# First attention: one bank pair for scores, two for transposed scores, values once per pair of heads

## The reference, cut to what matters

```python
h = concatenate([tokens(x), txt], axis=1)
h = h + attention16(layernorm(h))        # the stage that is changed most
h = h + recurrence(layernorm(h))         # gated recurrence over the batches, in order
h = h + gated_scan(layernorm(h));  h = h + quantised_mlp(layernorm(h))
h = h + masked_attention(layernorm(h));  h = h + top1_experts(layernorm(h))
h = h + alibi_attention(layernorm(h));   h = h + capacity_experts(layernorm(h))

# the first attention: 16 heads of width 16
xn = layernorm(x) * g + b
q, k, v = xn @ Wq + bq, xn @ Wk + bk, xn @ Wv + bv
attn = einsum('bnhd,bmhd->bnmh', q, k) / sqrt(16)
y = einsum('bnmh,bmhd->bnhd', softmax(attn, axis=2), v)
```

## Time and profile before

| | us |
|---|---|
| median of 3 runs | 2595.54 |
| lowest, highest run | 2593.53, 2599.7 |
| profiled execution, its time | 2592.93 |
| profiled execution, its span | 2591.0 |
| first attention, main loop | 207.6 to 638.2 |
| TensorE busy, share of the span | 1877.0 (72%) |
| DVE busy, share of the span | 1153.2 (45%) |
| TensorE clock granted, mean over the span | 0.886 |

### The profile page before, as it was taken

How to read it: one execution, slowest core, us unless ns; L and a number is a source line. 1 busy time by engine, 2 the same in 40 slices (tenths; PEclk the granted TensorE clock), 3 DMA queues, 4 the chain that set the end, 5 groups by cost and what they waited for, 6 DMA issues and landing times. The chain is left out here.

```text
span 2591.0 us, 33680 instructions
## 1 busy us (share of the span) xinstructions
PE 1877.0 (72%) x9606; PEld 1224.2 (47%) x9607; DVE 1153.2 (45%) x3544; ACT 750.1 (29%) x1842; POOL 487.2 (19%) x631
## 2 busy tenths in 40 slices
PE   0026399998995857876885299970899998984798
PEld 0013144443664546654554166650466665663576
DVE  2434276676225556654443011115566565661111
ACT  0002144444321102211221022210666555660221
POOL 0020010010001022210002500005344343452012
PEclk9999699999998979877995599995799888996899
DMA  9224455351002000003000400004000000001342
GB/s 199 76 47 143 99 102 91 64 106 22 0 0 55 0 0 1 0 1 162 0 0 0 150 29 28 28 21 134 1 7 18 14 15 15 17 18 35 108 141 78
DMA packets 75136, 131.23 MB, mean 51 GB/s; under 512 B 25670, under 2 KB 63202, under 8 KB 70686
## 3 DMA queue, kind: packets, MB, share of 16 engines
q1 hardware_dynamic: 49786, 106.58, 16.2%
q0 software_dynamic: 20512, 14.29, 2.4%
q10 hardware_dynamic: 4722, 9.09, 1.2%
HBM read 90.74 MB, written 40.13 MB: 51 GB/s over the span
## 5 line engine op out<-in xcount | busy, mean ns | idle before, releaser
L2117 POOL TENSOR_SCALAR l_P<-l_P,l_ri 111x111 f32<-111x111 f32 (+1 forms) x256 | 179.9, 721 | 232.9 <-DVE l_ri L2294 232.6
L622 ACT ACTIVATE PT<-psT 111x666 f32<-111x666 f32 x192 | 139.4, 726 | 220.3 <-PE psT L703 219.9
L523 DVE TENSOR_REDUCE mx<-psS 111x2 f32<-111x666 f32 x192 | 159.8, 848 | 88.2 <-PE psS L688 88.1
L2384 ACT ACTIVATE l_P<-l_S,l_nm 111x111 f32<-111x111 f32 (+2 forms) x384 | 179.2, 472 | 30.3 <-DVE l_nm L2287 30.0
L1231 PE MATMUL q_psY<-q_wq,q_xT 128*111 128x256 f32 x576 | 153.8, 426 | 2.1 <-ACT q_xT L1190 1.6
L714 PE MATMUL psO<-PT,vS 111*32 111x333 f32 x768 | 149.0, 467 | 0.1
L2504 PE MATMUL l_psP<-ident,l_P 111*111 111x111 f32 x768 | 108.1, 280 | 40.9 <-DVE l_PT L2303 39.8
L1827 DVE COPY t_hT<-t_psG 128x512 f32<-128x512 f32 x56 | 36.1, 686 | 214.3 <-PE t_psG L1869 214.3
L2504 PEld LDWEIGHTS l_psP<-ident,l_P 111*111 111x111 f32 x768 | 93.9, 187 | 71.9 <-DVE l_PT L2303 42.1
L1231 PEld LDWEIGHTS q_psY<-q_wq,q_xT 128*111 128x111 f32 x576 | 112.7, 202 | 31.0 <-issue 2.5
L1880 PE MATMUL t_psY<-expert_w,t_hT 128*128 x448 | 105.5, 389 | 18.6 <-DVE t_hT L1827 18.6
(11 more groups left out here) (378 smaller groups left out, 3697.8 us busy)
## 6 DMA issues: line engine op xcount, KB each, us to landing
expert_w<-in_moe_dram SPq DMA_DIRECT2D x8, 2048.0 KB, 15.1
c_w<-in_moe_dram SPq DMA_DIRECT2D x16, 1024.0 KB, 7.2
qs<-halves_scratch SPq DMA_DIRECT2D x128, 83.5 KB, 3.3
ks<-halves_scratch SPq DMA_DIRECT2D x128, 83.5 KB, 4.2
halves_scratch<-high SPq DMA_DIRECT2D x32, 167.0 KB, 4.1
halves_scratch<-low SPq DMA_DIRECT2D x32, 167.0 KB, 4.7
c_xb<-xs_scratch SPq DMA_DIRECT2D x8, 667.3 KB
xs_scratch<-zeros SPq DMA_DIRECT2D x6, 777.0 KB
```

The lines of the kernel that those rows point to most:

```text
L523: v.tensor_reduce(mx[J % 2][:, t, c:c + 65:64], psS[s % 2][0:TT, :, 0:T], AX.X, ALU.max, negate=True).then_inc(max_done, 1)
L622: s_.activation(PT[jp % 2][:, :, a, :], psT[0:TT, :, 0:T], ACT.Exp).then_inc(exp_done, 1)
L2117: r = g.tensor_scalar(Pt, Pt, ri[:, c % 2, 2 * t + half:2 * t + half + 1], None, ALU.mult)
L2384: s_.activation(P[c % 4][:, half, at(t):at(t + 1)], Sm[:, half, at(t):at(t + 1)], ACT.Exp, bias=nm[:, c % 2, i:i + 1], scale=-1.0, accum_o ...
```

## The change

The edit has five parts.
1. In the first attention the six banks of scores are shared out anew: one pair for scores, two for transposed scores. Scores of step s now wait for the maximum of step s - 1, and transposed scores of step s for the exponential of step s - 2.
2. `values` is called once for each pair, at steps with s % 3 = 1, for all three tiles of the pair before.
3. `AT` is written anew so that pieces stand at s % 3 = 1 (ahead of the transposed scores) and s % 3 = 2 (behind them), on TensorE and on ScalarE. `oS` has two buffers, and its copy comes a step later.
4. The zeros, their memset and their DMAs move to `recurrence`.
5. In the ALiBi attention the list of pieces is reordered, `route_rows` moves behind the pieces of chunk 4, and a drain is added ahead of `batch_stats`.

```diff
@@ attention16
-        oS = sb("oS", [128, T])
+        oS = [sb(f"oS{i}", [128, T]) for i in range(2)]
-        zeros = sb("zeros", [128, 1792])
-        psS = [pb2(f"psS{i}") for i in range(2)]
-        psT = pb2("psT")
+        ps = [pb2(f"ps{i}") for i in range(3)]
...
-        AT = [(1, "x", 0), (2, "x", 1), (3, "qk", 0), (4, "qk", 1), (5, "most", 1), (6, "ot", 3), (7, "qk", 2),
-              (8, "qk", 3), (9, "ot", 0), (11, "most", 2), (12, "v", 0), (13, "v", 1), (15, "ot", 1), (17, "most", 3),
-              (21, "ot", 2), (23, "most", 0)]
+        AT = [(1, "x", 0), (2, "x", 1), (4, "most", 1), (5, "qk", 0), (7, "qk", 1), (8, "ot", 3), (10, "most", 2),
+              (11, "ot", 0), (13, "qk", 2), (14, "qk", 3), (16, "most", 3), (17, "ot", 1), (19, "v", 0), (20, "v", 1),
+              (22, "most", 0), (23, "ot", 2)]
...
+        def score_bank(s):
+            return ps[0]
+        def less_bank(s):
+            return ps[1 + s % 2]
@@ SP
             batch(0, 0)
-            sync.wait_ge(zeros_ready, 1)
-            n = 0
-            for f in fills:
...
-            sync.wait_ge(filled, n)
@@ ScalarE
-                    if s == 1 and not first:
+                    if s == 2 and not first:
                         out(b - 1, 3)
-                    if s % 6 == 1 and s > 1:
+                    if s % 6 == 2 and s > 2:
                         out(b, s // 6 - 1)
-                    for args in pieces(b, p, s, first, last):
-                        piece(*args)
+                    if s % NT == 1:
+                        for args in pieces(b, p, s, first, last):
+                            piece(*args)
                     exp(b, s)
+                    if s % NT != 1:
+                        for args in pieces(b, p, s, first, last):
+                            piece(*args)
@@ TensorE
-                if some(NS * b + s - 1):
-                    pe.wait_ge(max_done, NS * b + s - 1)
+                if some(NS * b + s):
+                    pe.wait_ge(max_done, NS * b + s)
...
-                if some(NS * b + s):
-                    pe.wait_ge(exp_done, NS * b + s)
+                if some(NS * b + s - 1):
+                    pe.wait_ge(exp_done, NS * b + s - 1)
...
-            def values(b, p, s):
-                jp, a = s // NT, s % NT
-                pe.wait_ge(exp_done, NS * b + s + 1)
-                if s % 6 == 0 and some(4 * b + jp // 2):
+            def values(b, p, jp):
+                pe.wait_ge(exp_done, NS * b + NT * jp + NT)
+                if jp % 2 == 0 and some(4 * b + jp // 2):
                     pe.wait_ge(o_out, 4 * b + jp // 2)
-                for half in range(2):
...
-                if a == NT - 1:
-                    r.then_inc(pv_done, 1)
+                for a in range(NT):
+                    for half in range(2):
...
+                r.then_inc(pv_done, 1)
...
                     if s + AHEAD < NS or not last:
                         scores(*of(b, p, s + AHEAD))
-                    if s >= 2:
-                        values(b, p, s - 2)
-                    elif not first:
-                        values(b - 1, 1 - p, NS + s - 2)
-                    for args in pieces(b, p, s, first, last):
-                        piece(*args)
+                    if s % NT == 1:
+                        if s > NT:
+                            values(b, p, s // NT - 1)
+                        elif not first:
+                            values(b - 1, 1 - p, NPAIR - 1)
+                        for args in pieces(b, p, s, first, last):
+                            piece(*args)
                     scores_less_most(b, p, s, first, last)
+                    if s % NT != 1:
+                        for args in pieces(b, p, s, first, last):
+                            piece(*args)
@@ recurrence
+            nc.gpsimd.memset(zeros[:, :], 0.0).then_inc(zeros_ready, 1)
+        @block.sync
+        def _(sync):
+            sync.wait_ge(zeros_ready, 1)
+            n = 0
+            for f in fills:
...
+            sync.wait_ge(filled, n)
@@ alibi_attention
-        AT = [(0, "x", 0), (1, "x", 1), (2, "k", 0), (3, "k", 1), (4, "q", 0), (5, "out", 0), (6, "q", 1),
-              (7, "out", 1), (8, "q", 2), (9, "out", 2), (10, "q", 3), (12, "q", 4), (13, "v", 0), (14, "rx", 0),
-              (15, "rx", 1), (16, "rl", 0), (17, "v", 1), (18, "rk", 0), (19, "q", 5), (20, "v", 2), (21, "q", 6),
-              (22, "q", 7)]
+        AT = [(0, "x", 0), (1, "x", 1), (2, "k", 0), (3, "k", 1), (4, "out", 0), (5, "q", 0), (7, "out", 1),
+              (8, "q", 1), (10, "out", 2), (11, "q", 2), (12, "q", 3), (13, "v", 0), (14, "q", 4), (15, "rx", 0),
+              (16, "rx", 1), (17, "rl", 0), (18, "q", 5), (19, "v", 1), (20, "rk", 0), (21, "q", 6), (22, "v", 2),
+              (23, "q", 7)]
...
-                    if c == 4 and not first:
-                        route_rows(b - 1)
...
                     if c == 3 and not first:
+                        dve.drain()
                         batch_stats(nc, dve, sh, b - 1).then_inc(h_done, 1)
+                    if c == 4 and not first:
+                        route_rows(b - 1)
```

More of the change, by code:

```diff
@@ L323, in token_scale, with attention16 @@
     g.tensor_tensor(r, r, b, ALU.mult).then_inc(done, 1)
-def attention16(nc, sh, fills):
+def attention16(nc, sh):
     H, DH = 16, 16
@@ L490, in _ @@
             c.then_inc(consts, 1)
-            g.memset(zeros[:, :], 0.0).then_inc(zeros_ready, 1)
             def lower(b, n):
@@ L522, in largest @@
                 dve.wait_ge(s_done, NS * b + s + 1)
-                v.tensor_reduce(mx[J % 2][:, t, c:c + 65:64], psS[s % 2][0:TT, :, 0:T], AX.X, ALU.max,
+                v.tensor_reduce(mx[J % 2][:, t, c:c + 65:64], score_bank(s)[0:TT, :, 0:T], AX.X, ALU.max,
                                 negate=True).then_inc(max_done, 1)
@@ L674, in piece @@
                     for t in range(NT):
-                        r = nc.tensor.transpose(psM[0:TT, 128 * t:128 * t + 128], oS[:, qt(t)], sh.ident[:, :])
+                        r = nc.tensor.transpose(psM[0:TT, 128 * t:128 * t + 128], oS[j % 2][:, qt(t)], sh.ident[:, :])
                 r.then_inc(piece_done, 1)
@@ L683, in scores @@
                         pe.wait_ge(stack_in[n], 128 * (b + 1))
-                if some(NS * b + s - 1):
-                    pe.wait_ge(max_done, NS * b + s - 1)
+                if some(NS * b + s):
+                    pe.wait_ge(max_done, NS * b + s)
                 for half in range(2):
                     ph = slice(64 * half, 64 * half + 64)
-                    r = mm(psS[s % 2][0:TT, half, 0:TE], qs[p][ph, jp, qt(t)], ks[p][ph, jp, :], start=True, stop=True)
+                    r = mm(score_bank(s)[0:TT, half, 0:TE], qs[p][ph, jp, qt(t)], ks[p][ph, jp, :], start=True, stop=True)
                 r.then_inc(s_done, 1)
@@ L730, in body, with recurrence @@
                         scores(*of(b, p, s + AHEAD))
-                    if s >= 2:
-                        values(b, p, s - 2)
-                    elif not first:
-                        values(b - 1, 1 - p, NS + s - 2)
-                    for args in pieces(b, p, s, first, last):
-                        piece(*args)
+                    if s % NT == 1:
[5 more added lines that the diff above has]
+                            piece(*args)
                     scores_less_most(b, p, s, first, last)
+                    if s % NT != 1:
+                        for args in pieces(b, p, s, first, last):
+                            piece(*args)
                 if last:
-                    values(b, p, NS - 2)
-                    values(b, p, NS - 1)
+                    values(b, p, NPAIR - 1)
                     piece(*tail())
             batches(pe, body)
-def recurrence(nc, sh):
+def recurrence(nc, sh, fills):
     with ExitStack() as ctx:
@@ L759, in recurrence @@
         ps_tmp = sb("r_tmp", [TT, 2, NTILES])
+        zeros = sb("r_zeros", [128, 1792])
+        zeros_ready, filled = sem("r_zeros_ready"), sem("r_filled")
         ps = [pb(f"r_ps{i}") for i in range(8)]
@@ L771, in _ @@
             token_scale(nc, pool, sh, ps_tmp, "plain", scaled)
+            nc.gpsimd.memset(zeros[:, :], 0.0).then_inc(zeros_ready, 1)
[4 more added lines that the diff above has]
+            for f in fills:
+                parts = 128 if f.shape[0] % 128 == 0 else TT
+                flat = f.rearrange("(p r) c -> p (r c)", p=parts)
+                for a in range(0, flat.shape[1], 1792):
+                    m = min(1792, flat.shape[1] - a)
+                    sync.dma_start(flat[:, a:a + m], zeros[0:parts, 0:m]).then_inc(filled, 16)
+                    n += 16
+            sync.wait_ge(filled, n)
         @block.vector
@@ L2760, in program @@
             tokenise(nc, sh, ins, h0)
-            attention16(nc, sh, [xs, xs2[0:E * CAP, :]])
-            recurrence(nc, sh)
+            attention16(nc, sh)
+            recurrence(nc, sh, [xs, xs2[0:E * CAP, :]])
```

20 lines of the change are left out of this document (10 added, 10 removed).

## The result

The changed kernel takes 2642.09 us (median of 4 runs, 2640.1 to 2647.5) against 2594.53 for the kernel before beside it (4 runs, 2587.2 to 2599.7). The ratio is 1.0189, with a 95% interval of 1.0159 to 1.0218: 48 us slower, where 2656 was forecast. The profiled execution took 2647.5 us with a span of 2645.5, so against that of before it is 54.5 longer.

A forecast was written before the change was run, and what follows sets the result against it. TensorE was taken to bound the first attention before, the scores-maximum chain after. First attention +43, clock +27 and ALiBi -10 gave +60: 2653 us for the profiled execution, 2656 for the median, range 2600 to 2705.

The forecast's parts named there:

- The bound and the hole: First attention: TensorE bounds a middle batch of 45.5 us; the 59.9 us hole from SP's zero writes goes, at cost 0.
- One bank pair, the walk of the groups: First attention: scores wait for the preceding step's maximum; groups of three steps sum to 59.4 us a batch against 45.5.
- The loop ends: First attention: at three loop ends DVE stands 2.83 us before the norm, now on the path: +8.4 us.
- The clock: First attention: TensorE's idle gaps lower its clock, 3.4 us of low level twice a batch, 1.7 lost each: +27 us.
- The whole of the first attention: The stage takes 473.4 us against 430.6, +43, and the clock's fall adds +27.
- The ALiBi attention: Later router rows and reordered pieces gain 0.6 us a batch, 2.3 with a clock fall: -10, bounds +5 and -33.
- The sum: Whole kernel: +43 + 27 - 10 = +60 us, 2653 for the profiled execution and 2656 for the median.
- Rival 1: First attention: the scores chain binds but the clock stays up: +33, 2629 us; chance 0.18.
- Rival 2: First attention: clock as in the quantised stage (+46) and stacks late by 4 us a batch (+28): 2703 us; chance 0.16.
- Rival 3: First attention: DVE's work fits under the values block, TensorE's 42 us sets the batch: 2508 us; chance 0.13 including half-way.
- Its other leg: First attention: one values block in place of three is a gain, since changing the tiling mode drains TensorE; 1.9 against 2.22 us.
- Rival 4: Recurrence: nothing of the zeros is won, since their writes block that stage; they would have to last over 175 us there.

The follow-up runs named there:

- run 1: The kernel before with only the zeros, their memset and their DMAs moved to the recurrence: 2528.44 us, ratio 0.9762.
- Runs 6: version 3 with one bank pair for scores and its wait as the only further edit: 2550.32 us, ratio 0.9839.
- run 7: The changed kernel with the old list of places (`AT`) in the first attention; banks, waits and values block as changed: 2576.86 us, ratio 0.9931.
- run 9: The changed kernel with one more VectorE memset behind the maximum at each step with s % 3 = 2: 2656.21 us, ratio 1.0261.
- run 8: The kernel before with only `route_rows` moved behind the pieces of chunk 4 in the ALiBi attention: 2600.75 us, ratio 1.0024.
- run 12: version 3 with values once for each pair of heads and the copy of the result one step later: 2530.93 us, ratio 0.9778.
- version 3: The kernel before with the zeros moved and the ALiBi edit, the first attention's order as before: 2503.67 us, ratio 0.9647.
- run 4: The changed kernel with two bank pairs for scores and one for transposed scores again; values once per pair and places as changed: 2557.37 us, ratio 0.9863.

## Why the prediction was right, point by point

**The bound and the hole: right.** The 59.9 us of the zeros went, and went whole (run 1: 66). Their cost in the recurrence is nothing, as put.

**One bank pair, the walk of the groups: right in mechanism, and within 0.5 us in every group whose values block stayed fast.** The timeline of the batch above gives, in the order of the prediction, forecast first:

| group at step | forecast | measured | |
|---|---|---|---|
| 1 (x, x) | 5.47 | 7.24 | block at the lower clock |
| 4 (maxima, q) | 7.22 | 7.23 | |
| 7 (k, output with statistics) | 10.08 | 9.68 | |
| 10 (maxima, output) | 6.81 | 9.27 | block at the lower clock |
| 13 (k, q) | 7.77 | 9.28 | block at the lower clock |
| 16 (maxima, output) | 6.81 | 6.80 | |
| 19 (v, v) | 7.45 | 7.41 | |
| 22 (with norm and loop end) | 7.78 + 2.83 | 11.04 | |

Each measured number is the difference of two starts of L686. The forecasts make 62.2 and the batch 67.95 us. Three groups (steps 4, 16 and 19) came to within 0.05 us, two are 0.4 off: step 7 takes 9.7 and 10.1 us in turn from batch to batch, on either side of the 10.08, and the last group came 0.43 longer. Where step 13's block was fast, in another batch (505.79 to 513.42), its group took 7.63. The values block is 1.88 against 1.9. (The terms of step 7 add up to 10.05 and those of step 19 to 7.42, 0.03 less than the prediction writes; that changes nothing.) Runs 6, 7 and 9 confirm the mechanism from three sides: one pair alone costs 36 to 49 us, a VectorE instruction behind a maximum costs its own length in the group of step 16 and nothing where VectorE waits anyway, and the statistics and output piece cost nearly nothing where a values block follows.

**The loop ends: two and not three.** The prediction put 2.83 us for each of three loop ends, 8.4. VectorE stood so ahead of the norm only twice, in the kernel before (5.6 us in all) as in the changed one (6.1). The groups around these two ends took 11.04 and 10.83 us, against 7.91 where no loop ends: 6.0 in all.

**The clock: right in kind, too small.** I took two stretches of 3.4 us at 1.2 GHz a batch, 6.8 us, and 1.7 us of loss for each; no row of before stands behind the two numbers. This batch has three slow blocks, and against the forecast they cost 1.77 + 2.46 + 1.51 = 5.7 in place of 3.4. Its granted clock was 0.87 over 68.0 us, which makes, as an estimate, 2 x 0.13 x 68 = 18 us at 1.2 GHz: much more of it than I took, each microsecond of it at a lower price, since TensorE waits through a part of it. Batches 1 to 5 have two, three, four, two and three slow blocks. Over the stage, the window's clock of 0.88 lies in the range I gave. The mean of five batches, x piece to x piece ((608.13 - 277.44) / 5), is 66.1, against 59.4 + 3.4 + 1.4 for the loop ends, which is 64.2.

**The whole of the first attention.** Forecast +43 and +27, together +70; the recurrence starts 730.2 - 650.8 = 79.4 later. Up to the last transposed scores it is 507.6 us (207.6 to 715.2), where 473.4 + 27 = 500.4 was forecast: the term of the clock was too small by more than these 7.2, since the loop ends took 2.4 less than put. The remaining 2.4 us lie behind the stage's last scores (15.0 us to the recurrence, before 12.6).

**The ALiBi attention: the term that was mis-sized.** I gave it -10, within +5 and -33. From the first weight load of its x piece to the end of the kernel, the last expert layer included, it is 26 us shorter: that load starts at 1877.5 in place of 1796.9, 80.6 later, and the span grew by 54.5 only. What I had priced, 1.4 of a wait less 0.8, is there (l_psP's waits fall from 24.7 to 15.9 in 400 us, and `out` waits 6.9 for `l_oT`). What I made too small is the clock: "2.3 where a fall of the clock goes too" was the sentence, and -10 is about the middle between no fall and one in each of the seven batches. In the changed kernel's own 400 us, shifted by the 81 us, the windows say 0.98 in place of 0.93:

```profile
1961.00:2361.00 400.00, 358.88 (x2476) 246.76 (x2475) 269.06 (x1115) 251.69 (x865) 188.62 (x247) 0.98 0.07 17
```

The waits of TensorE don't carry the gain: those listed for these two windows come to 41.6 us before and 40.1 after. The clock is large enough to: 0.93 and 0.98 make, as an estimate, 2 x 0.07 x 400 = 56 and 2 x 0.02 x 400 = 16 us at 1.2 GHz, and 40 us less of it is worth up to 20. That the clock stays up because the waits for the turned copies got shorter is argued, and no run shows it by itself. I had also ascribed the gain to the move of the rows; by run 8 that gives none without the new place of rx.

**The sum.** +79.4 and -26.1 are +53 for the profiled execution (1.2 more lie between the stages), where +60 was forecast; the medians differ by 48. Two terms off by ten and by sixteen, with opposite signs, made the total look better than its parts; that much of it was luck.

**The rivals.** Rival 1 (the clock stays up) fails on the clock rows. Rival 2's late stacks aren't there: in the whole stage TensorE waited once for a stack, 2.3 us. Rival 3 needed a batch under 53 us, and the batches took 66.1. Its other leg, a block that saves time, is tested by run 12: to have the values in one block is no gain even with two score pairs. Rival 4 (nothing of the zeros is won) fails by run 1. The Trainium skill (TensorEngine Tiling, Key Properties) says that a change of the tiling mode drains TensorE, which would have one block be cheaper than three; the trace agrees on the block itself (1.81 us from its start to that of the next matmul, 345.33 to 347.14, against 3 x 0.74 = 2.22), and run 12 shows that this is lost again, with more, to the exponential. The Trainium skill (TensorEngine Tiling, PSUM Bottleneck) says that copying out of PSUM may become the bottleneck once tiling has made TensorE four times faster. This case is not quite that: VectorE was busy for 34.17 of the batch's 68.00 us, so its capacity was no limit; what cost the 115 us ahead of L686 was the order of its work, with one bank pair to hand over.

**What the new order costs, by its parts** (start of the recurrence, less version 3's 589.5): one score pair alone 36.4; values in a block alone 23.8; both, with two transposed pairs and old places, 73.4 (run 7); the new places on top 67.3, which makes 140.7. Each is good to some 6 us; the medians give 49, 34, 76 and 62. What stays open is run 4's last 31 us over run 12 (19 by the medians): its new places cost something with two score pairs as well, and I haven't taken apart how much of it is the ends of the loop.

## What to carry to other kernels

When a buffer between two engines goes from two to one, an instruction of the reader that stands between two reads goes onto the path wherever the writer then waits for that read (some 60% of run 9's memsets did), and a trace in which that reader is busy for only three quarters of the time doesn't show it: walk the order of both engines from one hand-over to the next. Long work of the reader then belongs right ahead of the writer's longest block of other work, and not behind it. Merging that work into one block saves its change-overs, but here it took cover away from a wait that the separate pieces had hidden; and before a consumer is moved to be later, look where its own first reader stands.

## What the runs showed of the hardware

A wait of TensorE's costs more than its length where the clock falls behind it. In the batch shown, the blocks behind waits of 1.93, 3.68 and 1.60 us took 3.24 to 3.54 us in place of 1.88, and those behind waits of 0.71 to 1.46 stayed at 1.88. The block behind the wait of 5.04 us at 405.71 took 3.40. The length of the one wait doesn't settle it: in the next batch, at 455.91, scores waited 1.46 us and the block behind them took 2.70.

Twelve value matmuls in a row take 1.81 us up to the start of the next matmul, and three groups of four between other matmuls 3 x 0.74: about 0.14 more for each group.
